# Sliding attention: order of the work in TensorE's slot, value products independent of the residual sum, and the output's bias copy moved to DVE

## The reference, cut to what matters

```python
h = tok(x)                      # top-k attention, feed-forward, convolution, max over token pairs: 32 x 125 x 128
h = h + attn(layernorm(h))      # sliding-window attention, 8 heads of 16, window of 32 tokens to either side
h = h + ffn(layernorm(h))       # reduces, for these inputs, to adding a layernorm
```

```python
qkv = x @ W_qkv + b_qkv
p   = softmax over |i-j| <= 32 of (q_i . k_j) / 4      # per head
out = (p @ v) @ W_proj + b_proj
```

## Time and profile before

| | us |
|---|---|
| median of 3 runs | 579.72 |
| lowest, highest | 578.99, 580.14 |
| profiled execution, its time | 579.02 |
| its span | 577.2 |
| PE busy in the span | 503.1 (87%) |
| DVE busy | 405.4 (70%) |
| ACT busy | 371.5 (64%) |
| POOL busy | 272.4 (47%) |

### The profile page before, as it was taken

The page is one execution under the profiler, slowest core; times in us unless marked ns, Lnnn a source line. Parts: engine busy times, 40 slices in busy tenths (PEclk is TensorE's granted clock), DMA queues, the critical chain, the costliest instruction groups (busy, mean ns, idle before and its releaser), DMA issues.

```text
span 577.2 us, 13845 instructions
## 1 busy us (share of the span) xinstructions
PE 503.1 (87%) x4554; PEld 351.9 (61%) x4554; DVE 405.4 (70%) x1694; ACT 371.5 (64%) x1115; POOL 272.4 (47%) x218
## 2 busy tenths in 40 slices
PE   6998999999995999999999999966888888888830
PEld 4677666666663577667766677634666666666510
DVE  3687678888863678787788787544777777777750
ACT  5874688899883445455444554446887888888740
POOL 3760577888775577676776767231111111111030
PEclk9999599999996999999999999986999999999955
DMA  4440212222220100010000000000000000000013
GB/s 155 144 141 23 58 44 58 59 65 64 60 78 21 35 19 18 24 33 19 19 19 27 28 2 0 2 0 1 2 1 2 2 2 2 2 2 2 2 41 103
DMA packets 21914, 19.87 MB, mean 34 GB/s; under 512 B 14180, under 2 KB 18436, under 8 KB 21716
## 3 DMA queue, kind: packets, MB, share of 16 engines
q1 hardware_dynamic: 21268, 18.28, 11.1%
q10 hardware_dynamic: 576, 0.71, 0.4%
HBM read 16.81 MB, written 2.18 MB: 33 GB/s over the span
## 4 chain that ended last, share of the span: by engine, by line
PE 39%; ACT 18%; DVE 5%; issue 3%; POOL 1%; DVEq 0%; ACTq 0%; POOLq 0%
ACT wprobs L977 11%; PE quad L807 9%; PE quad L784 9%; PE bank L829 6%; PE quad L852 3%; PE bank L909 3%; ACT wprobsT L1003 2%; PE quad L776 2%; ACT oF L995 2%; PE bank L858 2%; ACT woT L1010 2%; PE bank L798 1%; PE bank L822 1%; DVE n L1112 1%; PE bank L815 1%
## 5 line engine op out<-in xcount | busy, mean ns | idle before, releaser
L476 POOL TENSOR_SCALAR put<-keyb,c 100x1000 f32<-100x1000 bf16 x32 | 89.1, 2784 | 43.3 <-DMA keyb<-key_scratch 26.1
L1078 POOL TENSOR_TENSOR kbd<-wkT,c 128x250 f32<-128x250 f32 x32 | 19.3, 602 | 134.4 <-ACT wkT L985 134.4
L977 ACT ACTIVATE wprobs<-quad,wmax 125x125 f32<-125x125 f32 x256 | 73.1, 384 | 1.8 <-DVE wmax L1166 0.7
L1166 DVE CUSTOM_DVE_ANT_0 quad<-quad,c 125x125 f32<-125x125 f32 x256 | 65.7, 320 | 11.6 <-PE quad L852 8.0
L609 ACT ACTIVATE probs<-quad,negmax 100x250 f32<-100x250 f32 x128 | 58.4, 468 | 19.8 <-DVE negmax L561 18.7
L784 PE MATMUL quad<-h1T,w 128*128 128x500 f32 x128 | 61.8, 607 | 0.7 <-ACT hid L948 0.6
L807 PE MATMUL quad<-w,hid 128*125 128x128 f32 x512 | 58.8, 273 | 0.1
L807 PEld LDWEIGHTS quad<-w,hid 128*125 128x125 f32 x512 | 57.3, 188 | 0.8 <-issue 0.5
L491 PE MATMUL bank<-c,probs 100*125 100x100 f32 x256 | 46.3, 306 | 2.1 <-ACT probs L609 1.4
L948 ACT ACTIVATE hid<-quad,vec_cols 128x500 f32<-128x500 f32 x64 | 43.0, 676 | 7.2 <-PE quad L784 4.0
L491 PEld LDWEIGHTS bank<-c,probs 100*125 100x125 f32 x256 | 35.1, 200 | 19.5 <-issue 11.8
(11 more groups left out here) (138 smaller groups left out, 1193.8 us busy)
## 6 DMA issues: line engine op xcount, KB each, us to landing
keyb<-key_scratch SPq DMA_DIRECT2D x64, 97.7 KB
xa<-xT SPq DMA_DIRECT2D x8, 500.0 KB, 4.0
xt<-xtok SPq DMA_DIRECT2D x16, 250.0 KB
out<-o_all SPq DMA_DIRECT2D x4, 500.0 KB
w<-weights SPq DMA_DIRECT2D x1, 1024.0 KB, 7.1
vec_rows<-rows SPq DMA_DIRECT2D x1, 448.0 KB, 5.1
c<-consts ACTq DMA_DIRECT2D x1, 428.5 KB, 6.6
w<-weights ACTq DMA_DIRECT2D x1, 192.0 KB, 4.1
```

The costliest lines, as they stand in the source:

```text
L476: nc.gpsimd.tensor_scalar(put[u % 3][:, :, :], keyb[p][:, :, :], c[0:ROWS, CONST["sidx"]], None, ALU.is_equal).then_inc(put_done, 1)
L977: ins = nc.scalar.activation(probs[p][:, j, :], s_of(j), ACT.Exp, bias=negmax[p][:, j:j + 1], scale=-1.0)
L1166: ins = nc.vector.tensor_tensor_reduce(s_of(j), s_of(j), c[0:LH, CONST["band"]], 1.0, OFF, ALU.add, ALU.min, negmax[p][:, j:j + 1])
```

## The change

PE's order in a slot becomes: scores (clip u), transposes of heads 4 to 7 (clip u-1), the two `oT` transposes (now of clip u-2, made in the slot before as a product), keys and queries, values, the transpose of `otok` (clip u-2), transposes of heads 0 to 3, value products (clip u-1), projection (clip u-2). ACT copies `oT` of clip u-2 after the copy of the values and before the exponentials, and no longer makes `oF`. DVE makes the reciprocal and `otok` between heads 0 to 3 and heads 4 and 5, makes `oF` (as a tensor_scalar add) between heads 4 and 5 and heads 6 and 7, and takes the residual sum and its statistics to the end of the slot. `y_proj` moves onto columns 256 to 383 of the bank, over a part of `y_a`; the value products wait for `oF_done` in place of `z_done`, and the `oT` copy waits for `z_done` of the clip before.

```diff
--- before.py
+++ after.py
@@ -725,7 +725,7 @@
 
         s_bank, x_bank, t_bank, y_bank = banks[0:4], banks[4], banks[5:7], banks[7]
         x_k, x_q, x_v = x_bank[:, 0:LH], x_bank[:, 128:128 + LH], x_bank[0:LH, 256:256 + D]
-        y_a, y_of, y_proj = y_bank[0:LH, 256:512], y_bank[:, 0:LH], y_bank[0:LH, 128:128 + D]
+        y_a, y_of, y_proj = y_bank[0:LH, 256:512], y_bank[:, 0:LH], y_bank[0:LH, 256:256 + D]
 
         def s_of(head):
             return s_bank[head // 2][0:LH, LH * (head % 2):LH * (head % 2) + LH]
@@ -853,10 +853,6 @@
                                                kbd[p][CW * cc:CW * cc + CW, :, :].rearrange("p h l -> p (h l)"), start=True, stop=True)
                     ins.then_inc(scores, 1)
 
-                if within(u, 2, B + 2):
-                    pe.wait_ge(otok_done, u - 1)
-                    nc.tensor.transpose(y_of, otok[:, :], ident[0:LH, 0:LH]).then_inc(oF_ready, 1)
-
                 if within(u, 1, B + 1):
                     pe.wait_ge(exp_done, 4 * u)
                     wait(pe, pT1_done, u - 1)
@@ -867,8 +863,10 @@
                     ins.then_inc(pT1_ready, 1)
 
                 if within(u, 2, B + 2):
-                    pe.wait_ge(oF_done, u - 1)
-                    nc.tensor.matmul(y_proj, oF[:, :], w[:, WEIGHT["wp"]], start=True, stop=True).then_inc(proj_ready, 1)
+                    pe.wait_ge(oT_done, u - 1)
+                    for i in range(2):
+                        ins = nc.tensor.transpose(y_a[:, 128 * i:128 * i + 128], oT[:, LH * i:LH * i + LH], ident)
+                    ins.then_inc(otok_ready, 1)
 
                 if within(u, -2, B - 2):
                     wait(pe, qT_done, u + 2)
@@ -882,6 +880,10 @@
                     wait(pe, v_done, u + 1)
                     nc.tensor.matmul(x_v, n3T_all[:, LH * (u + 1):LH * (u + 1) + LH], w[:, WEIGHT["wv"]], start=True, stop=True).then_inc(v_ready, 1)
 
+                if within(u, 2, B + 2):
+                    pe.wait_ge(otok_done, u - 1)
+                    nc.tensor.transpose(y_of, otok[:, :], ident[0:LH, 0:LH]).then_inc(oF_ready, 1)
+
                 if within(u, 0, B):
                     pe.wait_ge(exp_done, 4 * u + 2)
                     wait(pe, pT0_done, u)
@@ -892,7 +894,7 @@
                     ins.then_inc(pT0_ready, 1)
 
                 if within(u, 1, B + 1):
-                    wait(pe, z_done, u - 1)
+                    wait(pe, oF_done, u - 1)
                     pe.wait_ge(pT0_done, u)
                     pe.wait_ge(pT1_done, u)
                     pe.wait_ge(v_done, u)
@@ -903,11 +905,9 @@
                                                vo[pm][:, j, :], probsT[pm][:, j, :], start=True, stop=True)
                     ins.then_inc(pv_ready, 1)
 
-                if within(u, 1, B + 1):
-                    pe.wait_ge(oT_done, u)
-                    for i in range(2):
-                        ins = nc.tensor.transpose(y_a[:, 128 * i:128 * i + 128], oT[:, LH * i:LH * i + LH], ident)
-                    ins.then_inc(otok_ready, 1)
+                if within(u, 2, B + 2):
+                    pe.wait_ge(oF_done, u - 1)
+                    nc.tensor.matmul(y_proj, oF[:, :], w[:, WEIGHT["wp"]], start=True, stop=True).then_inc(proj_ready, 1)
 
             in_turn(pe, ffn, window)
             for u in range(B, B + 2):
@@ -990,9 +990,10 @@
                     wait(act, pv_ready, u - 1)
                     nc.scalar.activation(vo[p][:, :, 0:HD], x_v.rearrange("p (h f) -> p h f", h=H), ACT.Copy).then_inc(v_done, 1)
                 if within(u, 2, B + 2):
-                    act.wait_ge(oF_ready, u - 1)
-                    wait(act, proj_ready, u - 2)
-                    nc.scalar.activation(oF[:, :], y_of, ACT.Identity, bias=col("wv_b")).then_inc(oF_done, 1)
+                    act.wait_ge(pv_ready, u - 1)
+                    wait(act, otok_ready, u - 2)
+                    wait(act, z_done, u - 2)
+                    nc.scalar.activation(oT[:, :], y_bank[:, 0:2 * LH], ACT.Copy).then_inc(oT_done, 1)
                 if within(u, 0, B):
                     wait(act, pT0_ready, u - 1)
                     exponents(0)
@@ -1004,10 +1005,6 @@
                 if within(u, 0, B):
                     exponents(2)
                     exponents(3)
-                if within(u, 1, B + 1):
-                    act.wait_ge(pv_ready, u)
-                    wait(act, otok_ready, u - 1)
-                    nc.scalar.activation(oT[:, :], y_bank[:, 0:2 * LH], ACT.Copy).then_inc(oT_done, 1)
 
             def root_z(lo, hi, count):
                 act.wait_ge(chain, count)
@@ -1170,29 +1167,32 @@
                     mask_and_max(0)
                     mask_and_max(1)
                 if within(u, 2, B + 2):
+                    dve.wait_ge(otok_ready, u - 1)
+                    wait(dve, otok_done, u - 2)
+                    nc.vector.reciprocal(rinv[:, :], y_a.rearrange("p (h f) -> p h f", h=H)[:, :, HD]).then_inc(rinv_done, 1)
+                    dve.wait_ge(rinv_done, u - 1)
+                    wait(dve, oF_ready, u - 2)
+                    nc.vector.tensor_tensor(otok[:, :].rearrange("p (h f) -> p h f", h=H),
+                                            y_a.rearrange("p (h f) -> p h f", h=H)[:, :, 0:HD],
+                                            rinv[:, :].unsqueeze(2).to_broadcast([LH, H, HD]), ALU.mult).then_inc(otok_done, 1)
+                if within(u, 0, B):
+                    mask_and_max(2)
+                if within(u, 2, B + 2):
+                    dve.wait_ge(oF_ready, u - 1)
+                    wait(dve, proj_ready, u - 2)
+                    nc.vector.tensor_scalar(oF[:, :], y_of, col("wv_b"), None, ALU.add).then_inc(oF_done, 1)
+                if within(u, 0, B):
+                    mask_and_max(3)
+                    dve.wait_ge(pT0_ready, u + 1)
+                    wait(dve, pv_ready, u - 1)
+                    nc.vector.tensor_copy(probsT[p][:, 0:4, :].rearrange("p h l -> p (h l)"), t_bank[0][0:LH, 0:4 * LH]).then_inc(pT0_done, 1)
+                if within(u, 2, B + 2):
                     dve.wait_ge(proj_ready, u - 1)
                     if u == 2:
                         dve.wait_ge(h0b_done, NP)
                     nc.vector.tensor_tensor(z_all[:, um2:um2 + 1, :], y_proj.unsqueeze(1), z_all[:, um2:um2 + 1, :], ALU.add).then_inc(z_done, 1)
-                if within(u, 0, B):
-                    mask_and_max(2)
-                    mask_and_max(3)
-                if within(u, 2, B + 2):
                     dve.wait_ge(z_done, u - 1)
                     nc.vector.bn_stats(zst[:, um2:um2 + 1, :].rearrange("p a b -> p (a b)"), z_all[:, um2:um2 + 1, :].rearrange("p a b -> p (a b)")).then_inc(stat, 1)
-                if within(u, 0, B):
-                    dve.wait_ge(pT0_ready, u + 1)
-                    wait(dve, pv_ready, u - 1)
-                    nc.vector.tensor_copy(probsT[p][:, 0:4, :].rearrange("p h l -> p (h l)"), t_bank[0][0:LH, 0:4 * LH]).then_inc(pT0_done, 1)
-                if within(u, 1, B + 1):
-                    dve.wait_ge(otok_ready, u)
-                    wait(dve, otok_done, u - 1)
-                    nc.vector.reciprocal(rinv[:, :], y_a.rearrange("p (h f) -> p h f", h=H)[:, :, HD]).then_inc(rinv_done, 1)
-                    dve.wait_ge(rinv_done, u)
-                    wait(dve, oF_ready, u - 1)
-                    nc.vector.tensor_tensor(otok[:, :].rearrange("p (h f) -> p h f", h=H),
-                                            y_a.rearrange("p (h f) -> p h f", h=H)[:, :, 0:HD],
-                                            rinv[:, :].unsqueeze(2).to_broadcast([LH, H, HD]), ALU.mult).then_inc(otok_done, 1)
 
             def spread(lo, hi, count):
```

## The result

| | before | after |
|---|---|---|
| median, us | 579.36 | 561.5 |
| lowest, highest | 578.79, 580.14 | 560.37, 564.65 |
| profiled execution, its time | 579.02 | 561.54 |
| its span | 577.2 | 559.8 |
| period of a `window` slot | 4.87 | 4.315 |

The changed kernel is faster: ratio 0.970, with a 95% interval of 0.966 to 0.974 (4 runs of each). In a later comparison (11 runs of before, 5 of after) it was 562.51 against 579.77, 0.971 (0.968 to 0.973). The prediction was 562.8.

A forecast was written before the change was run, and what follows sets the result against it. No engine full; a loop from scores through masks, exponentials, `oT` and L909 sets 4.87 us. At 4.33 over 29 periods, with slot 2's earlier start, 16.4 off 579.02 gives 562.6, median 562.8; range 556.5 to 568.5.

The forecast's parts named there:

- The new period: In a `window` slot: 4.33 us between scores in place of 4.87, from loops of 4.30 and 4.35.
- the hop from the exponentials' end to the scores: On PE at a slot's end: scores start 0.05 us after the exponentials end.
- the exponentials' end: On ACT: last exponentials end 4.25 us after the scores start, 0.15 late behind DVE's mask of heads 6 and 7.
- PE's loop: PE's slot end: heads 0 to 3 transposes, products, projection, next scores; period 4.17 to 4.35 us.
- its own two loops: Slot period by the loop through DVE's last mask and the exponentials, 4.30 us, and by PE's chain, 4.35.
- `oF` on DVE: Bias copy on DVE takes 0.21 us of its queue, upper bound 0.38.
- The new waits: `z_all` waiting for the projection and `oT` for `z_all`: slack 0.1 us before the next mask, 0.2 for `oT`.
- the 0.25 added for the slow level: Start of slot 2: 0.25 us added after 400.88 because its scores may run partly at the slow clock.
- The tail: Exponentials' end to `factors`: 6.1 to 7.2 us against 6.79, between 0.7 gained and 0.4 lost; taken as nothing.
- the first rival: Slot loops don't bite: projection overlaps products, last mask in time; period 4.15 to 4.2, 558.4 or 557 us; chance 0.17.
- DVE's queue: Rival: DVE's queue becomes the bound, `oF` starting at 2.9; period 4.50 or 4.6, 568 to 570 us; chance 0.18.
- The clock: Rival: PE's granted clock falls to 0.50 in the stage; PE loop 6.1 us, about 614 in all; chance 0.04.

The follow-up runs named there:

- e2: Kernel before with only PE's order changed: the two `oT` transposes behind the next slot's scores; 589.32 us against 580.44, ratio 1.015.
- e9: Changed kernel with PE's waits for scores and value products reordered, so the first matmul carries the wait met last; 562.07 us, period 4.255.
- e7: Changed kernel plus an unused 125x128 add on DVE behind `oF`, ahead of the mask of heads 6 and 7; 566.99 us, period 4.515.
- e5: Changed kernel, unedited, run again beside three edited versions on one chip; 562.51 us, period 4.315.
- e11: Changed kernel, unedited, run beside the wait-order versions on one chip; 563.14 us, 0.968 of before, period 4.315.
- e10: Changed kernel with reordered PE waits and heads 0 and 1 transposes waiting only for the first exponential pair; 559.24 us, 0.962 of before.
- e6: Changed kernel with one PE wait split: heads 0 and 1 transposes wait only for the first pair of exponentials; 562.45 us, period 4.315.

## Why the prediction was right

*The bound.* Right. L909 and the `oT` copy ahead of the scores were the part of the loop that could go; e2 shows that its removal frees the scores, and that DVE's order decides whether this pays.

*The time.* 562.6 was worked out for the profiled execution, which took 561.54. Of the 1.0 between the two, 0.45 is the stretch ahead of slot 1, which the change does not touch; 0.31 is the scores of slot 2, 6.13 after those of slot 1 where 6.44 was taken, 0.16 the 29 periods, and 0.07 the last exponentials.

*The new period.* 4.33 predicted, 4.315 measured, but partly by luck, as two errors stand against each other. The first is the hop from the exponentials' end to the scores, priced at 0.05 from L909's single wait; it is 0.14, since `exp_done` is not the wait that the first matmul carries. The second is the exponentials' end, 4.25 predicted and 4.18 measured. The masks of heads 6 and 7 started 2.93 after the scores (2.91 predicted), but two things made less of it: the exponentials of heads 6 and 7 follow their mask by 0.62 and not by the 0.69 I took, a figure from an ACT that sat waiting, and the last one is shorter, 0.36 in place of 0.42. The group of four lasts 1.25 in place of 1.16, so the mask costs 0.09, not 0.15. With only the hop priced right the loop would have come out at 4.39, with only the exponentials' end right at 4.23. The sum 4.18 + 0.14 = 4.32 is the loop that ends last.

*PE's loop.* Predicted 4.17 to 4.35. The products start at 3.32 (3.30 predicted), the projection at 3.88 (between the two cases), the scores 0.44 behind it: 4.32, which looks like a tie with the first loop. But this 0.44 is the exponentials' wait and not PE's own spacing, which is 0.41 in e9; by it PE's loop would end at 4.29 (an estimate), after which only the exponentials' loop is left at 4.32. e7 says the same. The forecast lay between its own two loops, 4.30 and 4.35.

*`oF` on DVE.* It takes 0.27 to the next instruction and lasts 0.35; I had 0.21, with bounds of 0.21 and 0.38. The Trainium skill (VectorE: DVE Perf Modes, section "The DRAIN you can't avoid") has the next operation wait until the pipeline has emptied, which would hold DVE for the whole 0.35. The prediction quoted only that: the same paragraph goes on that a next operation "that is not held starts earlier". The trace agrees with that: the mask starts 0.08 before `oF`'s end.

*The new waits.* The slacks held: no mask waits behind `z_all` (0.15 of room, 0.1 predicted) and `oT` is in time, 0.58 ahead of the exponentials.

*Slots 1 and 2.* The scores of slot 2 start 6.13 after those of slot 1; 400.88 and 394.69 gave 6.19, and 6.44 with the 0.25 added for the slow level. They last 0.99, partly at the slow level, and slot 2 is 4.62 long. That the 0.25 shows in slot 2's length and not in its start makes no difference to the sum, but its size is not fixed: in e5 the granted clock rises to 1.00 0.03 after the start of its scores and the slot takes 4.33, in e11, the same kernel, 1.25 after it and the slot takes 4.83.

*The tail.* `factors` starts 6.75 after the exponentials' end, in the middle of the predicted 6.1 to 7.2; nothing gained.

*The rivals.* The loops do bite (4.235, the nearest to the 4.15 to 4.2 of the first rival, is reached only in e10, by another edit). DVE's queue holds the last loop, through its last mask, and e7 shows it at full price, but not at the 4.50 of the rival. The clock stayed at 1.00 from slot 3 to the last one with scores. The hop of 0.14 could not be read from the earlier trace rows, where L909 covers it; the 0.26 ahead of the products could, but the transposes cover it and I did not ask.

## What to carry to other kernels

When no engine is full, lay out the loop by asking at each start what ended just before it, and look for an instruction that stands in the queue ahead of the loop's own and has a wait of its own. Here moving it out paid only with the engine that consumes its result moved too (PE's move alone cost 1.5%, the whole gains 3%). When several waits guard one instruction, write the one that is met last first; on PE this took 0.06 off a slot of 4.315, and 0.08 with one wait split (e9, e10).

## What the runs showed of the hardware

PE's first matmul starts 0.05 us after the event that it waits for when its own weight load carries that wait, 0.14 after it when the wait stands in one separate instruction ahead, and 0.26 when it is in the first of two (changed kernel and e6); with the order turned round the 0.14 became 0.05 (e10). An instruction of 128x125 on DVE with a bias per partition takes 0.27 to the next start and 0.35 in all (`oF`, changed kernel), against 0.21 and 0.29 for an add of two tensors of 125x128 (`z_all`). An instruction that waits for the one ahead of it starts later: the statistics follow `z_all` by 0.33 (443.89 to 444.22, changed kernel), a mask without such a wait by 0.21.
